# Edge stage of a graph network: tile pairs that share a PSUM bank, and float32r parts in place of bfloat16 parts and float32

## The chip, the cores and the metric

The kernel runs on one core of a Trainium2 chip. The metric is the device time of one launch in microseconds (us); lower is better. Engines are named as in the profile: PE is TensorE (its matmuls), PEld its weight loads, DVE is VectorE, ACT is ScalarE, POOL is GpSimd and SP is SyncE.

## The reference

Two graph network layers run on N = 3125 nodes with 256 features and E = 50000 edges with 16 features each. The change touches the first:

```
h   = relu(layernorm(x))
m   = relu(concat(h[src], h[dst], edge_attr) @ mW1 + mb1)     # 50000 x 512
agg = segment_sum(m @ mW2 + mb2, src)                          # per source node
u   = relu(concat(h, agg) @ uW1 + ub1) @ uW2 + ub2
x   = x + h + u
```

The second layer is three graph convolutions (matmul, sum over neighbours, gelu) and a residual; the change does not touch its code.

## The kernel before

The kernel runs four stages one after the other, each a block in which every engine has an instruction stream of its own and the streams meet at semaphores.

1. `sort_and_embed` sorts the edges by block of 128 source nodes (25 blocks) and scatters them, 128 at a time, into a list in DRAM (`src_list`); a tile is 128 edges of one source block. It also computes A = h @ mW1[source rows] + mb1 and B = h @ mW1[target rows] for all nodes. B goes to DRAM, A stays in SBUF, cut into three bfloat16 parts per value (`a_part`).
2. `edge_mlp`, the stage that the change rewrites, walks over NT = 416 tiles. For tile t:
   - SP loads the edge rows, POOL gathers the 128 rows of B for the targets (`brow`, a ring of 8 buffers, freed by the add of eight tiles earlier).
   - DVE makes the one-hot of the edges' place in their source block, once in bfloat16 (`oh16`, L1017) and once in float32 (`oh32`, L1018).
   - PE transposes the one-hot and the edge features ("turn", L953 and L954), ACT copies both to SBUF (L984 and L986, `turned`).
   - PE computes the "edge" sum in a PSUM bank: features times weights (L962), then the transposed one-hot times the three parts of A (L964).
   - DVE adds the gathered rows of B (L1025, `pre`), ACT applies relu (L992, `hid`).
   - PE computes the "node" sum: one-hot (float32) times `hid` (float32), L971, which the trace shows as two matmul records; DVE adds it into the sum of the source block, `S` (L1011).

   PE's order per step is turn(t), edge(t-1), node(t-2). ACT's order is the copies of t, relu of t-1. DVE's order is the S add of t-4, the one-hots of t, the B add of t-2. `pTurn`, `pEdge`, `pNode`, `turned`, `pre` and `hid` have two buffers each. Before the first tile DVE sets all of `S` (12800 columns) to zero, L997.
3. `build_and_update` counts edges for the second layer in a dense matrix and runs the node update; it reads `S`.
4. `graph_layers` is the second layer.

Of the kernel before, what the change touches and what calls it, by code (L numbers as in the profile page):

```python
# [40 lines left out]
NT = -(-E // P) + NW  # L41
NS = -(-(NT + NW * (CHK - 1)) // 8) * 8
LT = NT + 2 + NW
FULL_TILES = -(-E // P)
# [14 lines left out]
assert COLS * P >= E and COLS * P - E <= 2 * P and BLOCKS * CH == COLS and NT % 16 == 0 and CHK * CW >= NW * P  # L59
# [8 lines left out]
def windows(nc, eng, tile_map, first, n):  # L68

    _, got = nc.values_load_multi_w_load_instructions(  # L70
        tile_map[0:1, first:first + n], engines=[eng.engine], min_val=0, max_val=NW - 1,
        skip_runtime_bounds_check_because="the map counts at most NW - 1 windows before a tile")
    return {first + k: w for k, w in enumerate(got)}
# [30 lines left out]
def sort_and_embed(nc, io, dr, keep):  # L104
# [3 lines left out]
    with ExitStack() as stack:  # L108
        g = Names(nc, stack)
        hi16 = [g.sb(f"hi16_{n}", [P, COLS], BF16) for n in range(2)]  # L110
        ck_i32 = g.sb("ck_i32", [P, COLS], I32)
        lo16 = [g.sb(f"lo16_{n}", [P, COLS], BF16) for n in range(2)]
        onehot_dst = g.sb("onehot_dst", [P, 2, NW, CH], BF16)
        FILL = (NT - FULL_TILES) * ROW
        early = keep.A[:, NW * 3 * HID - (WINS + CHK + 6) * COLS - 2 * (CH + 3) * BINS - 2 * FILL:NW * 3 * HID]
# [13 lines left out]
        ck = g.sb("ck", [P, COLS])  # L129
# [16 lines left out]
        start_x = g.sb("start_x", [1, 2, WINS, CHK])  # L146
# [4 lines left out]
        base_row = g.sb("base_row", [P, BINS])  # L151
        ck_i = g.sb("ck_i", [P, WINS, CHK], I32)
        ck_row = g.sb("ck_row", [P, BINS])
        step_i = g.sb("step_i", [P, NS], I32)
        step_f = g.sb("step_f", [P, NS])
# [6 lines left out]
        ended_w = ended[0:NW - 1, 0, 0:NT]  # L162
# [17 lines left out]
        last_f = g.sb("last_f", [1, NW])  # L180
        some_w = g.sb("some_w", [1, NW])
        spare = g.sb("spare", [1, NW])
        iota_i = g.sb("iota_i", [P, P], I32)
        bins_i = g.sb("bins_i", [P, BINS], I32)
# [5 lines left out]
        stats = g.sb("stats", [P, NW, 6])  # L190
# [4 lines left out]
        h = g.sb("h", [P, 2, D])  # L195
        hT = g.sb("hT", [P, 2, D])
        w1 = g.sb("w1", [P, 4, HID])
        b1 = g.sb("b1", [1, HID])
        rA = g.sb("rA", [P, HID])
# [3 lines left out]
        we_r = rA[0:EF, :]  # L203
# [55 lines left out]
        ra_ready = g.sem("ra_ready")  # L259
        a_mid = g.sem("a_mid")  # L260
# [10 lines left out]
        def a_part(w, k):  # L271
            return keep.A[:, w * (3 * HID) + k * HID:w * (3 * HID) + (k + 1) * HID]
# [4 lines left out]
        def _(sp):  # L277
# [10 lines left out]
            def load_feat(m):  # L288
# [17 lines left out]
            sp.dma_start(dr.src_list[:, FULL_TILES:NT, :], fill[:, :, :]).then_inc(filled, 16)  # L306
# [6 lines left out]
            sp.wait_ge(filled, 16)  # L313
            _, last = nc.values_load_multi_w_load_instructions(
                last_w[0:1, :], engines=[sp.engine], min_val=0, max_val=LT - 1,
                skip_runtime_bounds_check_because="a source block's last tile, or a spare one of its own")
            for w in range(0, NW, 2):
                sp.dma_start(dr.src_list[:, bass.ds(last[w], 1), :], fill[:, 0:1, :]).then_inc(last_filled, 16)
# [51 lines left out]
        def _(act):  # L370
# [23 lines left out]
            def middle_parts(k):  # L394
# [7 lines left out]
            act.wait_ge(filled, 16)  # L402
            _, last = nc.values_load_multi_w_load_instructions(
                last_w[0:1, :], engines=[act.engine], min_val=0, max_val=LT - 1,
                skip_runtime_bounds_check_because="a source block's last tile, or a spare one of its own")
            for w in range(1, NW, 2):
                act.dma_start(dr.src_list[:, bass.ds(last[w], 1), :], fill[:, 0:1, :]).then_inc(last_filled, 16)
            for k in range(BLOCKS):
# [14 lines left out]
                if odd == 0 and 0 <= s - 1 < NW:  # L423
                    w = s - 1
                    act.wait_ge(a_done, w + 1)
                    nc.scalar.copy(a_part(w, 0), pA[:, :]).then_inc(a_hi, 1)
                    act.wait_ge(ra_ready, w + 1)
                    nc.scalar.copy(a_part(w, 1), rA[:, :]).then_inc(a_mid, 1)
# [21 lines left out]
        def _(dve):  # L450
# [34 lines left out]
            v.tensor_scalar(spare[:, :], keep.iota[0:1, 0:NW], float(NT + 2), None, ALU.add).then_inc(consts, 1)  # L485
# [19 lines left out]
            dve.wait_ge(consts, 3 + CH)  # L505
# [20 lines left out]
            link(v.tensor_scalar(tiles_i[:, :], sum_all, float(P - 1), None, ALU.add))  # L526
            link(v.tensor_scalar(tiles_i[:, :], tiles_i[:, :], 7, None, ALU.arith_shift_right))
            link(v.tensor_copy(tiles_f[:, :], tiles_i[:, :]))
# [6 lines left out]
            link(v.scalar_tensor_tensor(out=last_f[:, :], in0=tiles_end[0:1, 0:NW], scalar=-1.0, in1=spare[:, :],  # L535
                                        op0=ALU.add, op1=ALU.subtract))
            link(v.tensor_scalar(some_w[:, :], tiles_f[0:1, 0:NW], 0.0, None, ALU.is_gt))
            link(v.tensor_tensor(last_f[:, :], last_f[:, :], some_w[:, :], ALU.mult))
            v.tensor_tensor(last_w[:, :], last_f[:, :], spare[:, :], ALU.add).then_inc(last_ready, 1)
            v.tensor_copy(bin_iota[:, :], bins_i[:, :]).then_inc(consts, 1)  # L540
            v.tensor_scalar(before16[:, :], keep.iota[:, :], part[:, 0:1], None, ALU.is_gt).then_inc(consts, 1)
            dve.wait_ge(consts, 5 + CH)
# [8 lines left out]
            dve.wait_ge(consts, 12 + CH)  # L551
# [94 lines left out]
            def tables(k):  # L646

                if k == 5:
                    link(v.tensor_tensor(diag_w[:, :], tiles_end[0:NW, 0:NW], keep.ident[0:NW, 0:NW], ALU.mult))
                    link(v.tensor_reduce(end_w[:, :], diag_w[:, :], AX.X, ALU.add))  # L650
                    v.tensor_scalar(ended_w, step_f[0:NW - 1, 0:NT], end_w[0:NW - 1, 0:1], None, ALU.is_ge
                                    ).then_inc(tables_ready, 1)
                if k == 7:
                    dve.wait_ge(tables_done, 1)
                    link(v.tensor_copy(keep.src_map[:, :], pH[0:1, 0:NT]))
# [65 lines left out]
            for k in range(BLOCKS):  # L721
# [16 lines left out]
                if odd == 0 and 0 <= s - 1 < NW:  # L738
                    w = s - 1
                    dve.wait_ge(a_hi, w + 1)  # L740
                    if w == 0:
                        dve.wait_ge(we_parts, 1)
                    v.tensor_tensor(rA[:, :], pA[:, :], a_part(w, 0), ALU.subtract).then_inc(ra_ready, 1)
# [17 lines left out]
        def _(pe):  # L761
# [47 lines left out]
            def tables(k):  # L809
                if k == 6:  # L810
                    pe.wait_ge(tables_ready, 1)
                    mm(pH[:, 0:NT], ones[0:NW - 1, :], ended_w, start=True, stop=True).then_inc(tables_done, 1)
# [17 lines left out]
            for k in range(BLOCKS):  # L830
                if k == 0:
                    pe.wait_ge(base_copied, 1)
                    pe.wait_ge(consts, 5 + CH)
                    before(0)
                    pe.wait_ge(consts, 6 + CH)
                if k == 2:
                    pe.wait_ge(consts, 12 + CH)
# [25 lines left out]
                if odd == 1 and 0 <= s < NW:  # L863
                    if s == 0:
                        pe.wait_ge(w_in, 48)
                    if s >= 1:
                        pe.wait_ge(ra_ready, s)
# [10 lines left out]
def edge_mlp(nc, io, dr, keep):  # L878


    with ExitStack() as stack:
        g = Names(nc, stack)
        S = keep.S
        T = 16
        LCS = T // LC
        rows = g.sb("rows", [P, LCS, LC, ROW])
        BR = 8
# [5 lines left out]
        oh16 = g.sb("oh16", [P, 4, P], BF16)  # L893
        oh32 = g.sb("oh32", [P, 4, P])
        turned = g.sb("turned", [P, 2, 2 * P], BF16)
        pre = g.sb("pre", [P, 2, HID])
        hid = g.sb("hid", [P, 2, HID])
# [4 lines left out]
        s_zero = g.sem("s_zero")  # L902
# [8 lines left out]
        hid_ready = g.sem("hid_ready")  # L911
        node_done = g.sem("node_done")
        s_added = g.sem("s_added")
        GRP = 8
# [27 lines left out]
        def _(pe):  # L942
            mm = nc.tensor.matmul
            win = windows(nc, pe, keep.src_map, 0, GRP)

            for t in range(NT + 2):
                j = t % T
                if inside(t, NT):

                    pe.wait_ge(oh_ready, 2 * t + 2)  # L950
                    if t >= 2:
                        pe.wait_ge(turn_copied, t - 1)
                    nc.tensor.transpose(pT[j % 2][:, 0:P], oh16[:, j % 4, :], keep.ident16[:, :])  # L953
                    nc.tensor.transpose(pT[j % 2][0:EW, P:2 * P], rows16[:, j // LC, j % LC, 4:4 + EW],  # L954
                                        keep.ident16[:, :]).then_inc(turn_done, 1)
                if inside(t - 1, NT):
                    b = (t - 1) % 2
                    pe.wait_ge(turn_copied, t)
                    if t >= 3:
                        pe.wait_ge(pre_ready, t - 2)  # L960
                    w = win[t - 1]
                    mm(pE[b][:, :], turned[0:EW, b, P:2 * P], keep.we[:, :], start=True, stop=False)  # L962
                    for k in range(3):
                        last = mm(pE[b][:, :], turned[:, b, 0:P], keep.A[:, bass.ds(w * (3 * HID) + k * HID, HID)],  # L964
                                  start=False, stop=(k == 2))
                    last.then_inc(edge_done, 1)
                if inside(t - 2, NT):
                    pe.wait_ge(hid_ready, t - 1)
                    if t >= 4:
                        pe.wait_ge(s_added, t - 3)  # L970
                    mm(pN[t % 2][:, :], oh32[:, (t - 2) % 4, :], hid[:, t % 2, :], start=True, stop=True  # L971
                       ).then_inc(node_done, 1)
# [851 lines left out]
```

## Time and profile before

| | us |
|---|---|
| median of 3 runs | 2334.24 (2333.3 to 2336.12) |
| the profiled execution, its own time | 2332.68 |
| its span | 2330.9 |
| edge stage, first to last add into S | 600.94 to 1369.8 |

Of the span PE is busy 2022.8 us, DVE 1688.7, POOL 1178.0 and ACT 807.3. The busy time of an engine over the whole span is an average over four stages with different limits, so the stage has to be read by itself: a window inside it, and the order and the starts of its instructions on each engine. Matmuls overlap one another, so what one costs is the distance from its start to the next one's start, not its duration.

### The profile page before, as it was taken

How to read it: one execution, taken by the hardware profiler on the slowest of the kernel's cores; microseconds unless marked ns; L12 is line 12 of the kernel's file. 1: busy time of each engine (PE TensorE's matmuls, PEld its weight loads, DVE VectorE, ACT ScalarE, POOL GpSimd, SP SyncE). 2: the span in 40 equal slices, each digit the busy share in tenths (PEclk: the TensorE clock that was granted, in tenths of full speed). 3: DMA queues.
4: the chain of work that ended last, by engine and by line, in shares of the span. 5: the costliest groups of instructions: out<-in, count | busy, mean ns of one | idle time of the engine just before them, and what ended most of it. 6: DMA issues, size and time to landing. Idle time of an engine off the chain costs nothing. (4 is left out here: it accounts for less than half of the span.)

```text
span 2330.9 us, 37075 instructions
## 1 busy us (share of the span) xinstructions
PE 2022.8 (87%) x9567; PEld 1299.8 (56%) x9567; DVE 1688.7 (72%) x5368; ACT 807.3 (35%) x2430; POOL 1178.0 (51%) x1453
## 2 busy tenths in 40 slices
PE   4666766662799999999999989999977999999998
PEld 2333433331344444444444447777756898898897
DVE  7987776663899999999999977777764454454454
ACT  0222121110455555555555545555543201101100
POOL 3777777776555555555555549989862100000000
PEclk7677666665899999999999999999997999999999
DMA  4111111111555555555555541111122343343353
GB/s 115 46 46 46 46 45 46 46 45 33 146 155 158 156 157 156 156 157 156 158 156 158 156 150 60 60 56 60 62 67 74 99 138 108 91 138 108 99 144 109
DMA packets 185586, 242.59 MB, mean 104 GB/s; under 512 B 26333, under 2 KB 154266, under 8 KB 185387
## 3 DMA queue, kind: packets, MB, share of 16 engines
q0 software_dynamic: 45968, 119.96, 18.3%
q1 hardware_dynamic: 108258, 94.94, 14.1%
q10 hardware_dynamic: 31160, 25.32, 3.3%
q8 instruction: 90, 1.47, 0.3%
q14 instruction: 110, 0.89, 0.1%
HBM read 195.17 MB, written 44.86 MB: 103 GB/s over the span
## 5 line engine op out<-in xcount | busy, mean ns | idle before, releaser
L936 POOL DMA_INDIRECT brow<-B_rows,rows x416 | 396.4, 953 | 354.3 <-DVE pre L1025 343.5
L362 POOL DMA_INDIRECT src_list<-ring,ring_row x392 | 411.8, 1051 | 153.6 <-issue 116.8
L1706 PE MATMUL pO<-F,y 128*128 128x448 f32 x2100 | 455.7, 372 | 13.9 <-DVE y L1595 11.6
L971 PE MATMUL pNode<-hid,oh 128*128 128x512 f32 x832 | 430.4, 599 | 0.7 <-ACT hid L992 0.6
L1706 PEld LDWEIGHTS pO<-F,y 128*128 128x128 f32 x2100 | 394.6, 188 | 49.0 <-DVE y L1595 13.4
L992 ACT ACTIVATE hid<-pre 128x512 f32<-128x512 f32 x416 | 262.1, 630 | 342.3 <-DVE pre L1025 342.3
L1011 DVE TENSOR_TENSOR S<-S,pNode 128x512 f32 x416 | 286.1, 688 | 72.9 <-PE pNode L971 54.7
L964 PE MATMUL pEdge<-A,turned 128*128 x1248 | 338.8, 379 | 0.0
L1566 DVE CAST F<-raw 128x448 fp32r<-128x448 uint16 x525 | 204.4, 392 | 173.5 <-PE pO L1706 169.3
L1141 POOL TENSOR_SCALAR src_oh<-iota,src_s 128x128 bf16<-128x128 bf16 x473 | 304.5, 659 | 27.4 <-PE pC L1310 26.0
L1025 DVE TENSOR_TENSOR pre<-pEdge,brow 128x512 f32<-128x512 f32 x416 | 281.4, 676 | 3.4 <-PE pEdge L964 3.3
L795 PE MATMUL pP<-U,upto 128*128 128x182 bf16 x385 | 60.0, 322 | 161.3 <-DVE posf L557 161.1
L971 PEld LDWEIGHTS pNode<-hid,oh 128*128 128x128 f32 x832 | 136.8, 188 | 88.5 <-ACT hid L992 79.5
L1185 DVE TENSOR_SCALAR dst_oh<-iota_cw,dst_s 128x458 bf16<-128x458 f16 x568 | 183.0, 375 | 0.0
L964 PEld LDWEIGHTS pEdge<-A,turned 128*128 128x128 bf16 x1248 | 122.0, 98 | 101.2 <-issue 1.4
L1310 PE MATMUL pC<-dst_oh,src_oh 128*128 128x458 bf16 x568 | 157.8, 361 | 13.8 <-DVE dst_oh L1185 5.9
L962 PE MATMUL pEdge<-we_rows,turned 96*128 96x512 bf16 x416 | 159.0, 382 | 0.2 <-ACT turned L986 0.2
L795 PEld LDWEIGHTS pP<-U,upto 128*128 128x128 bf16 x385 | 42.9, 127 | 203.7 <-DVE posf L557 191.1
L1017 DVE TENSOR_SCALAR oh<-iota,rows 128x128 bf16<-128x128 bf16 x416 | 153.1, 368 | 0.9 <-DVE S L997 0.9
L1397 ACT CAST c_rows<-pC 128x458 uint16<-128x458 f32 x175 | 94.6, 540 | 155.1 <-PE pC L1310 150.5
L1018 DVE TENSOR_SCALAR oh<-iota,rows 128x128 f32<-128x128 f32 x416 | 146.1, 351 | 0.0
L953 PEld LDWEIGHTS pTurn<-ident,oh 128*128 128x128 bf16 x416 | 39.9, 96 | 177.4 <-DVE oh L1018 176.9
(280 smaller groups left out, 2914.6 us busy)
## 6 DMA issues: line engine op xcount, KB each, us to landing
raw<-C_rows SPq DMA_DIRECT2D x105, 560.0 KB, 3.8
C_rows<-c_rows ACTq DMA_DIRECT2D x175, 114.5 KB, 1.7
rows<-src_list SPq DMA_DIRECT2D x104, 100.0 KB, 2.4
brow<-B_rows,rows POOLq DMA_INDIRECT x416, 3.4
B_rows<-bst SPq DMA_DIRECT2D x25, 256.0 KB, 2.1
src_list<-ring,ring_row POOLq DMA_INDIRECT x392, 2.2
hT_rows<-hT SPq DMA_DIRECT2D x25, 128.0 KB, 1.8
resid<-in_x_dram SPq DMA_DIRECT2D x1, 3072.0 KB
```

What stands on the lines that cost most here:

```text
L362: nc.gpsimd.indirect_dma_start(dr.src_list[:, :, :].rearrange("p t w -> (p t) w"), bass.IndirectOffsetOnAxis(ap=ring_row[:, k % RING, t:t ...
L936: nc.gpsimd.indirect_dma_start(brow[:, t % BR, :], None, dr.B, bass.IndirectOffsetOnAxis(ap=rows_i[:, b, j, 1:2], axis=0)).then_inc(b_in[t ...
L962: mm(pE[b][:, :], turned[0:EW, b, P:2 * P], keep.we[:, :], start=True, stop=False)
L964: last = mm(pE[b][:, :], turned[:, b, 0:P], keep.A[:, bass.ds(w * (3 * HID) + k * HID, HID)], start=False, stop=(k == 2))
L971: mm(pN[t % 2][:, :], oh32[:, (t - 2) % 4, :], hid[:, t % 2, :], start=True, stop=True).then_inc(node_done, 1)
L992: nc.scalar.activation(hid[:, b, :], pre[:, b, :], ACT.Relu).then_inc(hid_ready, 1)
L1011: v.tensor_tensor(sw, sw, pN[j % 2][:, :], ALU.add).then_inc(s_added, 1)
L1025: v.tensor_tensor(pre[:, b, :], pE[b][:, :], brow[:, (j - 2) % BR, :], ALU.add).then_inc(pre_ready, 1)
L1141: nc.gpsimd.tensor_scalar(src_oh[:, s % SLOTS, :], keep.iota16[:, :], src_s[:, s:s + 1], None, ALU.is_equal).then_inc(src_ready, 1)
L1185: v.tensor_scalar(dst_oh[:, s % SLOTS, :], iota_cw[:, :], dst_s[:, s:s + 1], None, ALU.is_equal).then_inc(dst_ready, 1)
L1566: v.tensor_copy(F[:, n % FS, 0:CHUNK], raw[:, m % RAWS, n % RAWW, 0:CHUNK]).then_inc(f_ready, 1)
L1706: last = mm(pO[n % 2][half][:, 0:CHUNK], y_part(win, part, half), F[:, (n * NW + win) % FS, 0:CHUNK], start=(win == 0 and part == 0), stop ...
```

## The change

It does four things in the edge stage, and changes what lies around it to fit.

- A is kept in two float32r parts per value instead of three bfloat16 parts. PE's edge sum is then three matmuls, not four. `turned` is float32r, and the transposed edge features have a buffer of their own.
- Tiles go in pairs of the same source block. The node sums of both tiles accumulate in one PSUM bank, and DVE adds once per pair, with one instruction that multiplies the running sum by 0 or 1 (`going_on`) and adds the bank. So no large memset is needed. Each source block has an even number of tiles, and NT becomes 440.
- In every fourth tile (t % 4 == 1) relu is split into two float32r parts: ACT writes the upper part, DVE computes max(pre, 0) - upper, and the node sum is two float32r matmuls instead of one float32 matmul.
- DVE makes one one-hot per tile (float32r, 8 buffers). The transpose on PE reads the upper half of each 32-bit value, a bfloat16 with a step of two. PE's node sum runs one step later: turn(t), edge(t-1), node(t-3).

The first stage loses the middle part of A (one ACT copy and one DVE subtraction per source block) and writes its filler tiles with two DMAs instead of one. The third stage finds its weights in other places of SBUF and loads `uW1` with two DMAs instead of one.

```
-NT = -(-E // P) + NW
+PAIRS = E // (2 * P) + NW
+NT = 2 * PAIRS
...
-                    v.tensor_tensor(rA[:, :], pA[:, :], a_part(w, 0), ALU.subtract).then_inc(ra_ready, 1)
+                    v.tensor_tensor(a_part(w, 1), pA[:, :], a_part(w, 0).bitcast(F32), ALU.subtract).then_inc(a_lo, 1)
...
-                if odd == 1 and 0 <= s - 1 < NW:
-                    w = s - 1
-                    dve.wait_ge(a_mid, w + 1)
-                    v.tensor_tensor(a_part(w, 2), rA[:, :], a_part(w, 1), ALU.subtract).then_inc(a_lo, 1)
...
+            def turn(t):
+                pe.wait_ge(oh_ready, t + 1)
+                if t >= 2:
+                    pe.wait_ge(turn_copied, t - 1)
+                nc.tensor.transpose(pT[t % 2][:, 0:P], oh_upper[:, t % OHS, :, 1], keep.ident16[:, :])
+                nc.tensor.transpose(pT[t % 2][0:EW, P:2 * P], rows16[:, (t // LC) % LCS, t % LC, 4:4 + EW],
+                                    keep.ident16[:, :]).then_inc(turn_done, 1)
+
+            def edge(t):
+                pe.wait_ge(turn_copied, t + 1)
+                if t >= 2:
+                    pe.wait_ge(pre_ready, t - 1)
+                mm(pE[t % 2][:, :], turned_e[:, t % 2, :], keep.we[:, :], start=True, stop=False)
+                for k in range(2):
+                    last = mm(pE[t % 2][:, :], turned[:, t % 2, :],
+                              keep.A[:, 2 * HID + k * HID:][:, bass.ds(at[t // 2], HID)], start=False, stop=(k == 1))
+                last.then_inc(edge_done, 1)
+
+            def node(t):
+                pe.wait_ge(hid_ready, t + 1)
+                first, p = t % 2 == 0, t // 2
+                if first and p >= 2:
+                    pe.wait_ge(pair_added, p - 1)
+                if in_parts(t):
+                    mm(pN[p % 2][:, :], oh[:, t % OHS, :], upper[:, :], start=first, stop=False)
+                    pe.wait_ge(lower_ready, parts_upto(t))
+                    last = mm(pN[p % 2][:, :], oh[:, t % OHS, :], lower[:, :], start=False, stop=not first)
+                else:
+                    last = mm(pN[p % 2][:, :], oh[:, t % OHS, :].bitcast(F32), whole[(t % 4 + 1) // 2][:, :], start=first,
+                              stop=not first)
+                last.then_inc(node_done, 1)
...
+            for t in range(NT + 1):
+                if t < NT:
+                    act.wait_ge(turn_done, t + 1)
...
+                    nc.scalar.activation(turned[:, t % 2, :], pT[t % 2][:, 0:P], ACT.Copy,
                                          accum_out=keep.tile_deg[:, t:t + 1])
+                    nc.scalar.copy(turned_e[:, t % 2, :], pT[t % 2][0:EW, P:2 * P]).then_inc(turn_copied, 1)
+                u = t - 1
+                if u >= 0:
+                    act.wait_ge(pre_ready, u + 1)
...
+                    to = upper[:, :] if in_parts(u) else whole[(u % 4 + 1) // 2][:, :]
+                    nc.scalar.activation(to, pre[:, u % 2, :], ACT.Relu).then_inc(hid_ready, 1)
...
-            v.memset(S[:, :], 0.0).then_inc(s_zero, 1)
+            v.memset(keep.sums[:, 0:HID], 0.0).then_inc(start_ready, 1)
...
+            def lower_part(t):
+                dve.wait_ge(hid_ready, t + 1)
...
+                v.scalar_tensor_tensor(out=lower[:, :], in0=pre[:, t % 2, :], scalar=0.0, in1=upper[:, :].bitcast(F32),
+                                       op0=ALU.max, op1=ALU.subtract).then_inc(lower_ready, 1)
+
+            def add_pair(p):
+                dve.wait_ge(node_done, 2 * p + 2)
...
+                v.scalar_tensor_tensor(out=keep.sums[:, bass.ds(at[p], HID)],
+                                       in0=keep.sums[:, bass.ds(at[max(p - 1, 0)], HID)],
+                                       scalar=keep.going_on[:, p:p + 1], in1=pN[p % 2][:, :],
+                                       op0=ALU.mult, op1=ALU.add).then_inc(pair_added, 1)
+
+            one_hot(0)
+            for t in range(NT + 6):
+                if t + 1 < NT:
+                    one_hot(t + 1)
+                if 0 <= t - 2 < NT:
+                    add_target(t - 2)
+                if 0 <= t - 3 < NT and in_parts(t - 3):
+                    lower_part(t - 3)
+                if t >= 6 and t % 2 == 0:
+                    p = (t - 6) // 2
...
+                    add_pair(p)
...
-            sp.dma_start(uw1[:, :, :], io["L0_gnn_uW1"].rearrange("(k p) n -> p k n", p=P)).then_inc(w_in, 16)
+            for half in range(2):
+                sp.dma_start(uw1[:, 4 * half:4 * half + 4, :],
+                             io["L0_gnn_uW1"][:, half * D:(half + 1) * D].rearrange("(k p) n -> p k n", p=P)
+                             ).then_inc(w_in, 16)
```

## Rows read from the trace of the kernel before

**Rows 1.** Windows: each engine's busy time and instructions in a stretch, then PE's clock.

```profile
core 0: us, PE busy (x) PEld busy (x) DVE busy (x) ACT busy (x) POOL busy (x), PEclk, DMA share, GB/s
100.00:300.00 200.00, 142.44 (x618) 76.27 (x616) 158.62 (x759) 42.46 (x98) 155.18 (x148) 0.70 0.16 47
...
900.00:1100.00 200.00, 200.00 (x866) 89.35 (x866) 181.81 (x434) 111.66 (x435) 108.26 (x136) 1.00 0.56 157
...
1400.00:1736.00 336.00, 309.58 (x1870) 235.72 (x1868) 255.78 (x874) 180.34 (x333) 304.60 (x472) 1.00 0.19 60
```

**Rows 2.** Timeline of PE over one tile: start, duration, line, operation.

```profile
1000.79 0.22 PE L953 MATMUL pTurn<-ident,oh 128*128 128x128 bf16 x1
...
1000.90 0.38 PE L962 MATMUL pEdge<-we_rows,turned 96*128 96x512 bf16 x1
1001.12 0.81 PE L964 MATMUL pEdge<-A,turned 128*128 x3
1001.77 1.02 PE L971 MATMUL pNode<-hid,oh 128*128 128x512 f32 x2
1002.63 0.22 PE L953 MATMUL pTurn<-ident,oh 128*128 128x128 bf16 x1
```

**Rows 3.** Timeline of DVE over the same stretch and a little on.

```profile
1001.10 0.69 DVE L1011 TENSOR_TENSOR S<-S,pNode 128x512 f32 x1 [0.24 <-PE pNode L971]
1001.70 0.39 DVE L1017 TENSOR_SCALAR oh<-iota,rows 128x128 bf16<-128x128 bf16 x1
1001.86 0.29 DVE L1018 TENSOR_SCALAR oh<-iota,rows 128x128 f32<-128x128 f32 x1
1002.08 0.67 DVE L1025 TENSOR_TENSOR pre<-pEdge,brow 128x512 f32<-128x512 f32 x1
...
1005.85 0.67 DVE L1025 TENSOR_TENSOR pre<-pEdge,brow 128x512 f32<-128x512 f32 x1
1006.62 0.69 DVE L1011 TENSOR_TENSOR S<-S,pNode 128x512 f32 x1
```

**Rows 4.** Timeline of ACT over the same stretch.

```profile
1002.78 0.63 ACT L992 ACTIVATE hid<-pre 128x512 f32<-128x512 f32 x1 [0.85 <-DVE pre L1025]
1003.32 0.26 ACT L984 ACTIVATE turned<-pTurn 128x128 bf16<-128x128 bf16 x1
...
1003.57 0.25 ACT L986 COPY turned<-pTurn 96x128 bf16<-96x128 bf16 x1
```

**Rows 5.** Timeline of all engines at the start of the edge stage.

```profile
582.87 10.72 DVE L997 MEMSET S<- 128x12800 f32 x1 [34.92 <-issue]
583.78 0.96 POOL L936 DMA_INDIRECT brow<-B_rows,rows  x1 [0.30 <-issue]
...
595.72 0.25 ACT L986 COPY turned<-pTurn 96x128 bf16<-96x128 bf16 x1
...
596.03 0.61 PE L962 MATMUL pEdge<-we_rows,turned 96*128 96x512 bf16 x1 [0.25 <-ACT turned L986]
...
596.43 1.49 PE L964 MATMUL pEdge<-A,turned 128*128 x3
...
597.95 0.69 DVE L1025 TENSOR_TENSOR pre<-pEdge,brow 128x512 f32<-128x512 f32 x1 [2.26 <-PE pEdge L964]
```

**Rows 6.** Chain of waits, second layer: 25 float32r matmuls in a row.

```profile
1828.17 5.69 PE pT_g L1741 x25
```

**Rows 7.** Single lines: durations of one in ns, min/median/max, then the shapes.

```profile
L1741 PEld LDWEIGHTS pT_g<-y,pick x75: 187/188/188, 1827.8 to 2188.3; 128*128 128x128 f32 x75
```

**Rows 8.** Single lines with scalar_tensor_tensor on DVE, same columns.

```profile
L674 DVE SCALAR_TENSOR_TENSOR A<-A x1: 351/351/351, 136.6 to 136.6; 128x182 f32<-128x182 f32 x1
L1595 DVE SCALAR_TENSOR_TENSOR y<-pY,dis,y x75: 479/484/485, 1780.1 to 2181.6; 128x256 fp32r<-128x256 f32 x75
```

**Rows 9.** DMA issues by queue: count, size, median us from issue to landing.

```profile
brow<-B_rows,rows POOLq DMA_INDIRECT x416, 3.4
```

**Rows 10.** Timeline of SP at the start of the third stage.

```profile
1371.28 0.43 SPq L1243 DMA_DIRECT2D A<-in_L_gnn_uW_dram  x1
```

More of the change, by code:

```diff
@@ L65, in inside, with blocks_of @@
     return 0 <= t < n
-def windows(nc, eng, tile_map, first, n):
+def blocks_of(nc, eng, table, first, n):
     _, got = nc.values_load_multi_w_load_instructions(
-        tile_map[0:1, first:first + n], engines=[eng.engine], min_val=0, max_val=NW - 1,
-        skip_runtime_bounds_check_because="the map counts at most NW - 1 windows before a tile")
+        table[0:1, first:first + n], engines=[eng.engine], min_val=0, max_val=(NW - 1) * 2 * HID,
+        skip_runtime_bounds_check_because="the map counts at most NW - 1 source blocks before a pair of tiles")
     return {first + k: w for k, w in enumerate(got)}
@@ L312, in _ @@
             sp.wait_ge(last_ready, 1)
-            sp.wait_ge(filled, 16)
+            sp.wait_ge(filled, 32)
             _, last = nc.values_load_multi_w_load_instructions(
-                last_w[0:1, :], engines=[sp.engine], min_val=0, max_val=LT - 1,
-                skip_runtime_bounds_check_because="a source block's last tile, or a spare one of its own")
+                last_w[0:1, :], engines=[sp.engine], min_val=0, max_val=NT - 2,
+                skip_runtime_bounds_check_because="the first tile of a source block's last pair")
             for w in range(0, NW, 2):
-                sp.dma_start(dr.src_list[:, bass.ds(last[w], 1), :], fill[:, 0:1, :]).then_inc(last_filled, 16)
+                sp.dma_start(dr.src_list[:, bass.ds(last[w], 2), :], fill[:, 0:2, :]).then_inc(last_filled, 16)
             def store_b(w):
@@ L401, in _ @@
             act.wait_ge(last_ready, 1)
-            act.wait_ge(filled, 16)
+            act.wait_ge(filled, 32)
             _, last = nc.values_load_multi_w_load_instructions(
-                last_w[0:1, :], engines=[act.engine], min_val=0, max_val=LT - 1,
-                skip_runtime_bounds_check_because="a source block's last tile, or a spare one of its own")
+                last_w[0:1, :], engines=[act.engine], min_val=0, max_val=NT - 2,
+                skip_runtime_bounds_check_because="the first tile of a source block's last pair")
             for w in range(1, NW, 2):
-                act.dma_start(dr.src_list[:, bass.ds(last[w], 1), :], fill[:, 0:1, :]).then_inc(last_filled, 16)
+                act.dma_start(dr.src_list[:, bass.ds(last[w], 2), :], fill[:, 0:2, :]).then_inc(last_filled, 16)
             for k in range(BLOCKS):
@@ L911, in edge_mlp, with in_parts, parts_upto, before_same @@
         hid_ready = g.sem("hid_ready")
+        lower_ready = g.sem("lower_ready")
         node_done = g.sem("node_done")
-        s_added = g.sem("s_added")
-        GRP = 8
+        pair_added = g.sem("pair_added")
+        def in_parts(t):
+            return t % 4 == 1
+        def parts_upto(t):
+            return sum(in_parts(u) for u in range(t + 1))
+        def before_same(t):
+            return t - 2 if in_parts(t) and in_parts(t + 2) else t - 4
         block = stack.enter_context(nc.Block())
@@ L943, in _ @@
             mm = nc.tensor.matmul
[L944 to L972, printed above, removed]
-                if t % GRP == 0 and 0 < t < NT:
-                    win.update(windows(nc, pe, keep.src_map, t, GRP))
@@ L976, in _ @@
+            pe.wait_ge(start_ready, 1)
+            for t in range(NT + 3):
+                if t < NT:
+                    turn(t)
+                if 0 <= t - 1 < NT:
+                    edge(t - 1)
+                if 0 <= t - 3 < NT:
+                    node(t - 3)
+                if t % (2 * GRP) == 0 and 0 < t < NT:
+                    at.update(blocks_of(nc, pe, keep.pair_at, t // 2, min(GRP, PAIRS - t // 2)))
         @block.scalar
@@ L1030, in build_and_update @@
+            dve.wait_ge(pair_added, PAIRS)
 def build_and_update(nc, io, dr, keep):
```

242 lines of the change are left out of this document (119 added, 123 removed).

## The prediction

> **What bounds the kernel now.** I read the windows view first, because the share of busy time over the whole span mixes four stages. In the middle of the edge stage PE is busy all of 200 us at full clock, DVE 182, ACT 112, POOL 108 [rows 1]. PE makes eight matmuls per tile, so 866 in 200 us are 108.2 tiles, 1.848 us a tile, and 416 tiles take 768.8 us.
>
> Then the timeline of PE over one tile, for the distances between starts [rows 2]: two transposes 0.11, features 0.22, three parts of A 0.65 (0.217 each), node sum 0.86, next tile. That is 1.84 without a gap, so PE's own work is the bound. The edge sum is complete 0.16 after the node sum has begun (1001.12 + 0.81 = 1001.93 against 1001.77).
>
> DVE is close behind [rows 3]: from one start to the next 0.60 (S add), 0.16, 0.22 (one-hots), then the B add; after a B add the S add starts 0.77 later although the former lasts 0.67, so an operand at a register's address costs 0.10 more. ACT follows a B add after 0.70 (1002.08 to 1002.78) and needs 0.54 + 0.25 + 0.25 until both copies are done [rows 4].
>
> The first stage is bound by POOL: 155.2 us busy and 148 issues of 0.30 (the wait that stands before POOL's gather [rows 5]) fill 200 [rows 1].
>
> **The change, part by part.** S(t) is the start of PE's step t: turn(t), edge(t-1), node(t-3).
>
> *PE's own work.* 25 float32r matmuls of 512 columns take 5.69 us, 0.228 each [rows 6]; their weight load of 0.188 hides under them [rows 7]. Edge: 0.22 + 2 x 0.228 = 0.675 instead of 0.87. Node: 0.86 in three tiles of four, 2 x 0.228 = 0.455 in the fourth. A step is 0.11 + 0.675 + 0.86 = 1.645, the step with the parts (t % 4 == 0) is 1.24. Four steps make 6.175, or 1.544 a tile. The strided weight load of the transpose isn't in the trace; a slower one (0.19 as in [rows 7]) still lies under the node matmul before it, so I take nothing, at most 0.09 a tile.
>
> [...]
>
> *DVE's work.* Per four tiles: four one-hots (0.22), four B adds (0.60), one lower part, two pair adds. The last two are scalar_tensor_tensor. One over 182 columns of float32 from SBUF takes 0.351, which is 182 cycles at 0.96 per ns (0.19) plus 0.16; over 512 columns that makes 0.53 + 0.16 = 0.69. The one with a PSUM operand and a pointer takes 0.484 for 256, so 0.75 for 512 [rows 8]. The next instruction starts 0.09 before the end, as behind the S add (0.69, 0.60) [rows 3]. In all 0.88 + 2.4 + 0.60 + 2 x (0.66 + 0.10) = 5.4 of PE's 6.175. As a sum it fits.
>
> *The order on DVE doesn't fit.* In step 4 (any step with t % 4 == 0) its queue holds one_hot(5), add(2), lower(1), pair add, then in step 5 one_hot(6), add(3). Yet this is the step in which PE is fastest. Behind add(3) hangs relu(3) on ACT, and ACT takes the copies of tile 5 only after relu(3); edge(5) needs them. I follow this chain from S(3):
> - edge(2) done and seen by DVE: 0.11 + 0.675 + 0.16 = 0.945, plus 0.03 (matmul end 597.92, DVE 597.95 [rows 5]) = 0.975
> - add(2) to lower(1) 0.60; lower(1) to the pair add 0.69 + 0.10 = 0.79; to one_hot(6) 0.66; to add(3) 0.22
> - add(3) to relu(3) 0.70; relu and both copies 1.04; to PE 0.06 (595.97 to 596.03 [rows 5])
>
> The sum is 5.045. PE by itself would reach edge(5) after 1.645 + 1.24 + 1.645 + 0.11 = 4.64. So PE waits 0.405 in step 6, once in four tiles, and the next round starts from there: no other link is longer. relu(4) starts about S(3) + 5.0, its copies of tile 6 are ready near 6.1, and edge(6) comes at 6.7. The lower part is ready near S(3) + 2.3, PE asks at 2.65. Four tiles take 6.175 + 0.405 = 6.58, 1.645 a tile; **440 tiles take 723.8 us, 45.0 less** than 768.8, although they are 24 more.
>
> Bounds: with both scalar_tensor_tensor at the price of a plain add (0.60 to the next) the chain is 0.25 shorter: 1.583 a tile, 696.4. Upwards I know of DVE's register loads (five per eight tiles, not visible before, where eight were) and of the pair add's second register address; another 0.22 on the chain gives 1.70 a tile, 748.
>
> *The memset.* It lasts 10.72 for 12800 columns; for 512 it is 0.43. All of the stage's start hangs on it: from its end to the first B add are 4.4 us [rows 5]. The gathers don't take its place, since POOL's run beside the memset (tile 1 issued at 583.78 [rows 5]) and land after 3.4 [rows 9], before the new first add at about 587.7. **10.3 less.** If something else took over, the nearest candidate is that landing, 587.2, so nothing is lost.
>
> *Ends.* The node sum runs a step later and the last add is a pair's: 0.8 more (0 to 2). In the third stage one more DMA at SP lies before the weights that DVE and PE wait for, 0.43 [rows 10]: 0.5 more (0 to 1.5, its rows being shorter). The copies of A and the DVE work that leave the first stage are worth nothing, as POOL's scatter covers them; without that cover they would be 25 x 0.6 = 15 us of DVE. The second filler DMA at its start delays POOL by 1 at most, against four short DVE instructions fewer: nothing. POOL in the edge stage gets less time per tile (1.645 for a gather of 0.96 + 0.30) and still has room; the same for SP's loads, with eight tiles of B rows ahead.
>
> **Sum.** -45.0 - 10.3 + 0.8 + 0.5 = -54.0, against the profiled execution's own 2332.7: 2278.7, say **2279 us**. That execution is 1.6 below the median, which changes nothing. By the bounds the forecast case spans 2251 to 2303.
>
> **Rivals.**
> - *PE stays the bound.* DVE's sum is below PE's, and my chain is only 0.4 longer than PE's path; if ACT's or DVE's links are shorter when nothing waits, the stage runs at 1.544 to 1.58: 679.3 to 696, the kernel 2234 to 2251. For it: all links but one have room. Against it: every link is a row. Chance 0.18.
> - *DVE is later than the chain says.* Register loads in the queue, or a pair add that waits for the node sum and pushes the next one-hot. At 1.70 to 1.75 a tile: 2303 to 2325. Chance 0.18.
> - *The lower part costs twice as much and ends the gain.* If the instruction takes half an element a cycle, it lasts 1.22, the chain gets 0.53 longer, four tiles take 7.11, a tile 1.778, 440 tiles 782: 2337, on the line between no change and slower. It decides from 0.49 us more per four tiles on (1.768 a tile). The same for the pair adds too would be 0.53 more: 1.91, 840, so 2395. Against both: neither row of scalar_tensor_tensor shows half rate, 0.351 for 182 columns with both tensors in SBUF would have to be 0.54 [rows 8]. Chances 0.07 (0.04 of it no change, 0.03 slower) and 0.02. The Trainium skill states it as a rule (Vector Engine (DVE) Microarchitecture Reference, Points that are easy to get wrong): this instruction "with two non-bf16 SBUF sources halves throughput". The trace disagrees by that row, at 182 columns; it has none at 512.
> - *The clock falls.* With PE waiting, the granted clock could drop to 1.2 GHz as in the first stage (0.70 with PE busy 142 of 200); PE's 6.175 would double, 440 tiles take 1359: 2914. But in the third stage PE is busy 310 of 336 at 1.00 [rows 1], 92%, and here it would be 6.175 of 6.58, 94%. Chance 0.03.
>
> **How the numbers follow.** The forecast case has 0.52. Faster by over 0.2% (about what a measurement of this kernel tells from none): 0.52 + 0.18 + 0.18 = 0.88. Within 0.2%: 0.04. Slower: 0.03 + 0.02 + 0.03 = 0.08. The range of 8 in 10 takes the forecast case, the upper two thirds of the first rival and most of the second: 2240 to 2318.
>
> **What the changed profile would show.** PE about 94% busy in the stage, with one wait of some 0.4 us in four tiles, at the feature matmul of every tile with t % 4 == 1, released by ACT's copy. ACT's relu of t % 4 == 3 starts late after DVE. The lower part lasts 0.69, the pair add 0.75. The first B add comes near 588. PE fully busy would mean the first rival; waits at more places the second; a lower part of 1.2 the third. The prediction is wrong at its root if float32r matmuls start more than 0.23 apart, if the strided transpose shows, or if the first stage becomes longer.

## The result

| | before | after |
|---|---|---|
| median | 2335.2 (2333.3 to 2338.3, 4 runs) | 2258.15 (2256.8 to 2260.0, 4 runs) |
| span of the profiled execution | 2330.9 | 2254.8 |
| first to last B add | 768.5 (415 tiles) | 705.9 (439 tiles) |

The ratio is 0.967, interval 0.965 to 0.969: faster, 77 us. The forecast was 2279, the range 2240 to 2318.

The windows view of the changed kernel, same three stages as [rows 1], and one longer stretch of the edge stage:

```profile
core 0: us, PE busy (x) PEld busy (x) DVE busy (x) ACT busy (x) POOL busy (x), PEclk, DMA share, GB/s
100.00:300.00 200.00, 143.09 (x619) 76.78 (x617) 153.76 (x754) 35.86 (x87) 155.49 (x147) 0.69 0.16 47
900.00:1100.00 200.00, 199.59 (x876) 119.94 (x874) 167.25 (x344) 126.20 (x501) 130.73 (x157) 1.00 0.64 180
1320.00:1656.00 336.00, 309.61 (x1870) 235.84 (x1867) 254.93 (x874) 180.34 (x333) 305.25 (x472) 1.00 0.18 60
...
700.00:1200.00 500.00, 498.91 (x2184) 299.19 (x2182) 417.39 (x858) 314.74 (x1248) 327.02 (x390) 1.00 0.65 181
```

PE's and POOL's rows have changed only in the edge stage; DVE and ACT have a little less in the first. PE shows as busy nearly all the time, but this hides its wait: a matmul is counted until its modelled end, which covers a short gap before the next. The wait is in the starts. Timeline of PE over four tiles (the turn begins a step; L970 and L972 are the edge sum, L986 the whole node sum, L982 and L984 its two parts):

```profile
1001.09 0.22 PE L962 MATMUL pTurn<-ident,oh 128*128 128x128 bf16 x1
...
1002.74 0.22 PE L962 MATMUL pTurn<-ident,oh 128*128 128x128 bf16 x1
...
1003.54 0.39 PE L982 MATMUL pNode<-hid_upper,oh 128*128 128x512 f32 x1
1003.77 0.39 PE L984 MATMUL pNode<-hid_lower,oh 128*128 128x512 f32 x1
1004.00 0.23 PE L962 MATMUL pTurn<-ident,oh 128*128 128x128 bf16 x1
...
1005.66 0.22 PE L962 MATMUL pTurn<-ident,oh 128*128 128x128 bf16 x1
...
1005.95 0.39 PE L970 MATMUL pEdge<-we_rows,turned_e 96*128 96x512 bf16 x1
...
1007.50 0.22 PE L962 MATMUL pTurn<-ident,oh 128*128 128x128 bf16 x1
```

The steps are 1.65, 1.26, 1.66 and 1.84. In the last one the features' matmul begins 0.29 after the turn and not 0.11: 0.18 of wait at edge(5), where the prediction has it. The view of waits counts it (columns: engine, line and releaser; us in total, times, longest), over 700 to 1200, which holds 312 tiles:

```profile
DVE pre L1039 <- PE pEdge L972: 53.5, 116, 0.8
DVE sums L1054 <- PE pNode L986: 29.1, 39, 0.8
...
PEld pEdge L970 <- ACT turned_e L1010: 12.1, 76, 0.2
```

76 times is once in four tiles. DVE over the same stretch (L1030 one-hot, L1039 B add, L1045 lower part, L1054 pair add):

```profile
998.59 0.69 DVE L1039 TENSOR_TENSOR pre<-pEdge,brow 128x512 f32<-128x512 f32 x1
1000.03 0.75 DVE L1054 SCALAR_TENSOR_TENSOR sums<-sums,going_on,pNode 128x512 f32 x1 [0.75 <-PE pNode L986]
...
1002.09 0.69 DVE L1039 TENSOR_TENSOR pre<-pEdge,brow 128x512 f32<-128x512 f32 x1 [0.31 <-PE pEdge L972]
1002.69 0.68 DVE L1045 SCALAR_TENSOR_TENSOR hid_lower<-pre,hid_upper 128x512 fp32r<-128x512 f32 x1
1003.29 0.74 DVE L1054 SCALAR_TENSOR_TENSOR sums<-sums,going_on,pNode 128x512 f32 x1
1003.95 0.29 DVE L1030 TENSOR_SCALAR oh<-iota,rows 128x128 fp32r<-128x128 f32 x1
1004.15 0.68 DVE L1039 TENSOR_TENSOR pre<-pEdge,brow 128x512 f32<-128x512 f32 x1
```

This is the predicted queue, from the B add at 1002.09 to the B add at 1004.15. The distances from start to start are 0.60, 0.60, 0.66, 0.20; the prediction had 0.60, 0.79, 0.66, 0.22. ACT's copies for edge(5) end at 1005.90 (L1010, from 1005.65). The chain from 1001.09 to 1005.95 is 4.86, predicted 5.045. Ahead of the pair add at 1000.03 DVE is idle for 0.75, once in eight tiles (39 times above); the profile puts it down to the node matmul, though the last one before it had ended at 999.41 (L986, from 998.39). The experiments come back to that row.

The start of the edge stage, from the same kernel's timeline:

```profile
574.63 0.48 DVE L1022 MEMSET sums<- 128x512 f32 x1 [32.38 <-PEq L109]
...
576.89 1.01 POOL L948 DMA_INDIRECT brow<-B_rows,rows  x1 [0.15 <-issue]
...
580.34 0.69 DVE L1039 TENSOR_TENSOR pre<-pEdge,brow 128x512 f32<-128x512 f32 x1 [2.94 <-DMA brow<-B_rows,rows]
```

Where 76.1 us of span went, by four pieces that fill it:

| piece | before | after | difference | predicted |
|---|---|---|---|---|
| to the first stage's last scatter | 569.4 | 563.7 | -5.7 | 0 |
| from there to the first B add | 28.6 | 16.7 | -11.9 | -10.3 |
| to the last B add | 768.5 | 705.9 | -62.6 | -45.0 |
| to the end | 964.5 | 968.6 | +4.1 | +1.3 |

### The profile page after: what moved, and what is told of

Its sections match the earlier page's. It is cut to its first block and busy times, and to the rows that moved or that the text cites. A ratio compares the mean times of both kernels' runs of the same rounds, so it can differ in the third digit from the quotient of the medians.

```text
span 2254.8 us, 35599 instructions
## 1 busy us (share of the span) xinstructions
PE 1954.4 (87%) x9319; PEld 1379.4 (61%) x9319; DVE 1555.3 (69%) x4889; ACT 806.8 (36%) x2501; POOL 1219.9 (54%) x1483
## 5 line engine op out<-in xcount | busy, mean ns | idle before, releaser
L948 POOL DMA_INDIRECT brow<-B_rows,rows x440 | 439.4, 999 | 237.3 <-DVE pre L1039 211.9
L1753 PEld LDWEIGHTS pO<-F,y 128*128 128x128 f32 x2100 | 395.6, 189 | 48.1 <-DVE y L1642 13.5
L972 PE MATMUL pEdge<-A,turned 128*128 x880 | 360.3, 491 | 0.0
L1039 DVE TENSOR_TENSOR pre<-pEdge,brow 128x512 f32<-128x512 f32 x440 | 302.9, 688 | 81.9 <-PE pEdge L972 78.2
L986 PE MATMUL pNode<-hid_whole,oh 128*128 128x512 f32 x660 | 338.3, 594 | 0.2
L1017 ACT ACTIVATE hid_whole<-pre 128x512 f32<-128x512 f32 x330 | 208.6, 632 | 160.0 <-DVE pre L1039 159.9
L1054 DVE SCALAR_TENSOR_TENSOR sums<-sums,going_on,pNode 128x512 f32 x220 | 163.4, 743 | 42.2 <-PE pNode L986 42.0
L972 PEld LDWEIGHTS pEdge<-A,turned 128*128 128x128 f32 x880 | 170.3, 194 | 11.0 <-issue 0.2
L970 PE MATMUL pEdge<-we_rows,turned_e 96*128 96x512 bf16 x440 | 170.0, 386 | 2.9 <-ACT turned_e L1010 1.4
L395 ACT CAST ring<-feat 128x336 bf16<-128x336 f32 x56 | 26.3, 470 | 368.2 <-DMA src_list<-ring,ring_row 342.7
L986 PEld LDWEIGHTS pNode<-hid_whole,oh 128*128 128x128 f32 x660 | 125.0, 190 | 29.1 <-ACT hid_whole L1017 0.9
L962 PE MATMUL pTurn<-ident,oh 128*128 128x128 bf16 x440 | 98.1, 223 | 35.5 <-DVE oh L1030 35.5
```

The costliest lines, as they stand in the source:

```text
L948: nc.gpsimd.indirect_dma_start(brow[:, t % BR, :], None, dr.B, bass.IndirectOffsetOnAxis(ap=rows_i[:, b, j, 1:2], axis=0)).then_inc(b_in[t ...
L970: mm(pE[t % 2][:, :], turned_e[:, t % 2, :], keep.we[:, :], start=True, stop=False)
L972: last = mm(pE[t % 2][:, :], turned[:, t % 2, :], keep.A[:, 2 * HID + k * HID:][:, bass.ds(at[t // 2], HID)], start=False, stop=(k == 1))
L986: last = mm(pN[p % 2][:, :], oh[:, t % OHS, :].bitcast(F32), whole[(t % 4 + 1) // 2][:, :], start=first, stop=not first)
L1017: nc.scalar.activation(to, pre[:, u % 2, :], ACT.Relu).then_inc(hid_ready, 1)
L1039: v.tensor_tensor(pre[:, t % 2, :], pE[t % 2][:, :], brow[:, t % BR, :], ALU.add).then_inc(pre_ready, 1)
```

## The experiments

Ratios are to the kernel before on the same chip; "the stage" is the time from the first to the last B add in the profile, 705.9 in the changed kernel, 439 tiles.

**1. The parts at another place.** The tile whose relu is split is the one with t % 4 == 2, so that the lower part falls into a step without a pair add.

```
 def in_parts(t):
-    return t % 4 == 1
+    return t % 4 == 2
...
-    ... whole[(t % 4 + 1) // 2]
+    ... whole[(0, 1, 1, 2)[t % 4]]
```

> The split tile moves from t % 4 == 1 to t % 4 == 2, so that the lower part stands on DVE in a step without a pair add. Theory A (the chain edge(2), B add, lower part, pair add, one-hot, B add, relu, copies, edge(5), 4.86 us in the changed kernel's trace, holds PE up by 0.18 in four tiles): the longest chain is then 4.24 against PE's 4.69, no wait is left, four tiles take 6.24 instead of 6.42, 110 x 0.18 = 20 us less: 2238. Rival B (PE's own work or its weight loads make that gap): nothing changes, 2258. Rival C (DVE as a whole is the limit): nothing changes either, but the wait moves to another tile.

Measured 2260.3, ratio 0.969 (0.967 to 0.970); the stage 706.1. No gain where 2238 was expected: with the lower part and the pair add in different steps, something else holds PE too. The waits over 700 to 1200 and the place where it happens:

```profile
DVE sums L1054 <- issue: 29.1, 39, 0.8
...
PE pEdge L970 <- ACT turned_e L1010: 9.9, 39, 0.3
```

```profile
999.86 0.69 DVE L1039 TENSOR_TENSOR pre<-pEdge,brow 128x512 f32<-128x512 f32 x1 [0.17 <-PE pEdge L972]
1001.29 0.75 DVE L1054 SCALAR_TENSOR_TENSOR sums<-sums,going_on,pNode 128x512 f32 x1 [0.75 <-issue]
```

PE now waits 39 times and not 76, once in eight tiles, but longer: the turns lie at 1001.78, 1003.44, 1005.52, 1006.77, so one step is 2.08 where 1.66 is its own work. That is 0.42 in eight tiles, 55 times, 23 us. Ahead of it stands the same idle of 0.75 before a pair add, and here the profile names no releaser. In the code DVE loads five registers at this point, every fourth pair (`blocks_of` in DVE's loop); this is what the expectations call the burst. The trace has it as one instruction of DVE's sequencer (`DVEq`), which isn't counted as busy. The view of its line over 700 to 1200 in the changed kernel (duration in ns, min/median/max):

```profile
L71 DVEq TENSOR_LOAD <-pair_at x39: 1180/1183/1193, 703.6 to 1191.0; - x39
```

The one before the pair add at 1000.03 begins at 998.6 and lasts 1.18, so it ends 0.24 before that pair add and 0.4 after the node matmul. The row of the changed kernel was put down to the wrong cause. Here the load begins at 999.9 and ends 0.24 before the pair add as well. Four tiles take 6.23 from turn to turn where no such load stands and 6.65 where one does, so the theory is right in the rounds without a load.

**2. No parts.** `in_parts` returns False, `whole` has four buffers, and DVE's B add no longer waits for a lower part.

```
-    return t % 4 == 1
+    return False
...
-    ... whole[(t % 4 + 1) // 2]
+    ... whole[t % 4]
...
-                    dve.wait_ge(lower_ready, parts_upto(t - 2))
```

> No tile is split; all node sums are float32 matmuls, four buffers for relu's result. Theory A: PE's own work is 4 x 1.66 = 6.64 per four tiles and nothing waits: 0.22 more, 110 x 0.22 = 24 us more: 2282. If the split buys nothing, because PE then only waits: 2258.

Measured 2280.9, ratio 0.977 (0.975 to 0.978); the stage 729.4, 6.65 per four tiles, which is four times PE's 1.66.

```profile
700.00:1200.00 500.00, 499.56 (x2109) 292.76 (x2109) 366.06 (x754) 311.15 (x1207) 301.71 (x377) 1.00 0.61 174
```

PE is the bound, with 2 waits in 500 us. The parts are worth 22.8 us. The rest of the stage's gain fits A in two parts (PE's step is 1.66, and was 1.84); no run tests A alone.

**3. Parts in every second tile,** odd ones and even ones.

```
-    return t % 4 == 1
+    return t % 2 == 1        # the other run: t % 2 == 0
...
-    ... whole[(t % 4 + 1) // 2]
+    ... whole[t % 4 // 2]
```

> Every second tile is split (t % 2 == 1), so lower part and pair add stand together in every even step. PE's own work is 5.84 per four tiles. Theory A: the same chain now closes a loop of 5.98 (B add to edge(5) 3.86, edge(5) to edge(6) 1.25, to the B add 0.87), so 0.44 less than 6.42 and 48 us less: 2210. Rival C (DVE's sum, 5.72 per four tiles by the distances, is in truth larger): 6.2 or more, 2234 or above.

> Every second tile is split, but the even ones (t % 2 == 0), so lower parts and pair adds stand in different steps. PE's own work is 5.84, DVE's 5.72, both as in the run with odd tiles. Theory A: the longest chain is 4.13 against PE's 4.18, so PE is never held up: 5.84 per four tiles, 64 us less than the changed kernel: 2194. Rival C (only DVE's sum counts, not its order): the same time as the run with odd tiles.

Measured 2248.1 (ratio 0.963, 0.961 to 0.965) and 2237.5 (0.959, 0.957 to 0.960); the stage 694.4 and 686.6. Both are faster than the change, and both miss what the chain forecast, 2210 and 2194. The rival by which only DVE's sum counts had the same time for both, and they differ by 10.6. The turns show where the chain is right. With odd parts four tiles take 6.06 in the rounds without a burst (turns at 1003.26 and 1009.32; 5.98 expected) and 6.58 in those with one (996.68 to 1003.26); with even parts 5.87 (1002.71 to 1008.58; 5.84 expected) and 6.65 (996.06 to 1002.71). The waits of the even one:

```profile
DVE sums L1054 <- issue: 30.3, 40, 0.8
...
PE pNode L984 <- DVE hid_lower L1045: 20.8, 40, 0.5
```

Again DVE is idle for 0.76, 40 times, and again PE is late once in eight tiles, now at the node sum's second part.

**4. The registers loaded one at a time.** This tests the theory that the first experiment left: the load of five costs DVE 0.75. With the parts at t % 4 == 2, DVE loads one register per pair, in the odd steps, behind the one-hot.

```
+    if t % 2 == 1 and 0 <= t - 5 < NT:
+        at.update(blocks_of(nc, dve, keep.pair_at, (t - 5) // 2, 1))
     if 0 <= t - 2 < NT:
         add_target(t - 2)
...
-        if p % GRP == 0:
-            first = max(p - 1, 0)
-            at.update(blocks_of(nc, dve, keep.pair_at, first, min(p + GRP, PAIRS) - first))
```

> The parts at t % 4 == 2, as in the run of 2260, and DVE's register loads one at a time, each in an odd step ahead of the B add that waits for PE, where that run had five in a burst ahead of the pair add. Theory R (the burst keeps DVE for 0.75 us once in eight tiles, and with the parts at t % 4 == 2 PE waits for it): PE's own work is the bound again, 6.24 per four tiles, 20 us less: 2238 to 2242. Theory D (DVE has too much work in a row by itself, the loads cost what the trace shows as idle anyway): 2256 to 2262. If one load costs nearly what five cost together, two in four tiles would make it 2265 to 2275.

Measured 2238.1, ratio 0.958 (0.956 to 0.960); the stage 685.4, 6.245 per four tiles.

```profile
700.00:1200.00 500.00, 500.00 (x2250) 304.61 (x2249) 431.23 (x883) 332.46 (x1287) 336.97 (x402) 1.00 0.66 186
```

The idle before the pair add and PE's wait are gone from the list of waits, and four tiles take PE's own 6.24. The 22 us that experiment 1 had missed are here. Only the loads differ, in eight tiles four of one register in place of one of five: it was the burst. The same view of the loads, in this run and then in the kernel before, whose load was of eight registers:

```profile
L71 DVEq TENSOR_LOAD <-pair_at x161: 299/304/323, 700.6 to 1198.8; - x161
```

```profile
L70 DVEq TENSOR_LOAD <-src_map x33: 593/596/606, 711.4 to 1185.3; - x33
```

A load of one takes 0.30, of five 1.18 and of eight 0.60; PE's own, of four, takes 0.33 in the changed kernel. So it isn't a price per register, and why five are dearer than eight was not tested, nor a load of four or eight on DVE at this place.

**5. The burst on the chain.** The changed kernel with the burst two steps earlier, between the lower part and the pair add of the queue shown above.

```
-        if p % GRP == 0:
+        if p == 0 or p % GRP == GRP - 1:
```

> The changed kernel with the burst of register loads moved by two steps: it stands between the lower part and the pair add, in the chain on which edge(5) waits, instead of two steps from there. As many loads as before but one more in the first burst. Theory R (the 0.75 us of idle ahead of the pair add once in eight tiles are the loads, and the changed kernel hides them): now they lie on the chain, 55 times 0.75 = 41 us more than 2258: 2290 to 2299. Rival W (that idle is a wait for the node matmul, as the profile puts it down, and the loads cost next to nothing): 2256 to 2262.

Measured 2274.3, ratio 0.974 (0.972 to 0.976); the stage 725.9, 20 us longer. The rival without a cost falls; the size, 41 expected on top of 2258, was wrong by half. DVE where the burst stands, and the load there:

```profile
1010.82 0.69 DVE L1039 TENSOR_TENSOR pre<-pEdge,brow 128x512 f32<-128x512 f32 x1 [0.77 <-PE pEdge L972]
1011.43 0.68 DVE L1045 SCALAR_TENSOR_TENSOR hid_lower<-pre,hid_upper 128x512 fp32r<-128x512 f32 x1
1012.36 0.75 DVE L1054 SCALAR_TENSOR_TENSOR sums<-sums,going_on,pNode 128x512 f32 x1 [0.24 <-issue]
```

```profile
L71 DVEq TENSOR_LOAD <-pair_at x1: 1181/1181/1181, 1010.9 to 1010.9; - x1
```

The pair add starts 0.93 after the lower part, and 0.60 without a burst: 0.33 lost, not 0.75. The load begins 0.1 after the B add's start and ends at 1012.12, and the pair add starts 0.24 later, as in the changed kernel and in experiment 1. What differs is how much work DVE's array has meanwhile: here the B add and the lower part, there the B add alone, so it is idle for 0.24 here and for 0.75 there. 55 times 0.33 are 18 of the 20 us. The round without a burst takes 6.42 in this run (turns at 1003.41 and 1009.83). In the changed kernel every round does, with a burst or without (turns at 996.33, 1002.74 and 1009.16, the burst in the first; 12.86 per eight tiles over the stage), so there the burst costs nothing: it stands ahead of B adds that wait for PE anyway. The changed kernel without its burst was not measured.

**6. Both: parts in every even tile, loads one at a time.** The diffs of 3 and 4 together.

> The parts in every even tile, as in the run of 2237.5, with DVE's register loads one at a time in the odd steps. Per four tiles DVE has 4 x 0.22 + 4 x 0.60 + 2 x 0.60 + 2 x 0.66 = 5.80, PE has 5.8 too; that run took about 6.2. Theory R: without the burst (0.37 per four tiles) it comes down to 5.9 to 6.1 per four tiles: 2200 to 2225. Theory D (DVE is full and a single load costs about as much as the burst): no gain or a loss, 2236 to 2260.

Measured **2197.4**, ratio 0.941 (0.939 to 0.943); the stage 646.9, below the range expected.

```profile
1000.05 0.68 DVE L1039 TENSOR_TENSOR pre<-pEdge,brow 128x512 f32<-128x512 f32 x1
1000.65 0.68 DVE L1045 SCALAR_TENSOR_TENSOR hid_lower<-pre,hid_upper 128x512 fp32r<-128x512 f32 x1
1001.25 0.28 DVE L1030 TENSOR_SCALAR oh<-iota,rows 128x128 fp32r<-128x128 f32 x1
1001.52 0.69 DVE L1039 TENSOR_TENSOR pre<-pEdge,brow 128x512 f32<-128x512 f32 x1
1002.12 0.73 DVE L1054 SCALAR_TENSOR_TENSOR sums<-sums,going_on,pNode 128x512 f32 x1
...
1005.89 0.68 DVE L1039 TENSOR_TENSOR pre<-pEdge,brow 128x512 f32<-128x512 f32 x1
```

```profile
700.00:1200.00 500.00, 500.00 (x2393) 316.67 (x2391) 500.00 (x1025) 353.01 (x1366) 407.41 (x428) 1.00 0.70 197
```

Four tiles take 5.84 on DVE with no gap, and PE's own work is 2 x (1.66 + 1.26) = 5.84 as well; the mean of the stage is 5.89. Single loads, 0.30 each, cost nothing visible: they run while DVE's array is busy. This is the fastest version, 61 us below the change, and PE and DVE are both full. Against the version of experiment 3 the eight tiles are 12.51 - 11.79 = 0.72 shorter, the burst's idle.

**7. The start hangs on DVE.** Twenty more memsets of 512 columns in a chain ahead of the one that is left.

```
+    for n in range(20):
+        link(v.memset(keep.sums[:, 0:HID], 0.0))
     v.memset(keep.sums[:, 0:HID], 0.0).then_inc(start_ready, 1)
```

> Twenty more memsets of 512 columns stand ahead of the one on which the edge stage's start hangs, each behind the other. Together with the last one they are to last about 10 us (21 x 0.48), nearly as long as the one memset of the kernel before (10.72). Theory M (the edge stage's start came earlier because the memset is short): the time of 10 us comes back, 2268 against the changed kernel's 2258. Rival N (PE's or the gathers' start sets the first B add, and the long memset was hidden under the first gather for the most part): 2258 to 2262.

Measured 2267.5, ratio 0.971 (0.969 to 0.973): 9.4 more than the change. They take more than the 10 expected, as each starts 0.66 after the last: 578.86 to 592.50 in the timeline, 13.6. The first B add is released by PE again:

```profile
592.02 0.48 DVE L1025 MEMSET sums<- 128x512 f32 x1 [0.17 <-DVE sums L1024]
...
595.21 0.69 DVE L1042 TENSOR_TENSOR pre<-pEdge,brow 128x512 f32<-128x512 f32 x1 [2.04 <-PE pEdge L972]
```

From the last scatter to the first B add are 27.3, and 16.7 in the changed kernel. So 13.2 more of memset move the first B add by 10.6. The stage itself is 2.2 shorter (703.7; argued: the gathers are ahead by then), and the whole comes to 8.5, near the 9.4 of the medians.

**Without a time.** Four more runs were planned and gave no time: A's second part multiplied twice, which would price A on PE; the changed kernel with its registers loaded one at a time; and the kernel before for a second and a third profile. On the second question see the rounds in experiment 5; the others stay open.

## Why the prediction was right, and where it was off

**PE's own work: right.** Steps of 1.65 and 1.26 where 1.645 and 1.24 were forecast, 6.24 where 6.175; 0.065 in four tiles, 7 us too little over 440. The float32r parts start 0.23 apart (1003.54, 1003.77), and the strided transpose's weight load doesn't show. That PE alone makes 6.65 without parts is experiment 2.

**The order on DVE: the mechanism right, one term mis-sized.** PE waits at edge(5), once in four tiles, after the queue that the prediction lists. The term that failed is "lower(1) to the pair add 0.69 + 0.10 = 0.79"; measured 0.60. Two errors lie in it. The 0.10 came from the 0.77 between the B add and the S add in [rows 3], read as the price of a register's address. It was a wait. PE in the kernel before:

```profile
1005.44 1.03 PE L971 MATMUL pNode<-hid,oh 128*128 128x512 f32 x2
```

This node sum ends at 1006.47, and the S add starts 0.15 later, at 1006.62; in the four tiles before, the S add starts 0.14 or 0.15 after a node sum's end too. In the pair add, with two register addresses and no wait, nothing of the 0.10 is left. The 0.69 was the duration worked out from [rows 8] without the 0.09 by which the next instruction starts before the end, which the same paragraph had stated. With 0.60, and the others' small differences, the chain is 4.86 and the wait 0.18, not 0.405: 0.225 x 110 = 24.8 us less. Less 7.2 for PE's steps, this is 17.6, the whole difference between -45.0 and -62.6. The kernel so came out between the forecast case and its lower bound (2251), where this very term had been priced as a plain add.

**The lower part at half rate: refuted at 512 columns.** The row that the trace before did not have:

```profile
L1045 DVE SCALAR_TENSOR_TENSOR hid_lower<-pre,hid_upper x110: 680/682/685, 584.3 to 1284.9; 128x512 fp32r<-128x512 f32 x110
```

Both tensors are 32 bits wide and in SBUF, and it takes 682, against 688 of the B add. Against the rule cited from the Trainium skill (Vector Engine (DVE) Microarchitecture Reference, Points that are easy to get wrong), the measurement decides; 1.22 was its price.

**DVE later by its register loads: true as a mechanism, not in this kernel.** The prediction named the loads as an upward bound and in the second rival, and took five to be no more visible than the eight before. The load of five lasts 1.18 where that of eight lasted 0.60. It leaves DVE idle for 0.75 in eight tiles, and experiments 1 and 4 show what that can cost (22 us). That it costs nothing here is luck: the change happens to put it where DVE waits for PE.

**The memset: -10.3 forecast, -11.9 to the first B add.** Two terms that the prediction had at nothing lie in it. DVE reaches its memset sooner after the last scatter, 10.9 instead of 13.5 (cause open), and from the memset's end to the first B add are 5.2 instead of 4.4. The releaser is the gather (580.34, issued 576.89: 3.45), which the prediction had as "the nearest candidate" at no cost. In experiment 7, where PE is the last again, it is 2.7. Experiment 7 gives back 9.4 with a memset chain somewhat longer than the old memset. That some of the start's gain is lost again within the stage is read from one pair of profiles, not tested by itself.

**The first stage: 0 forecast, -5.7 in the two profiles, cause open.** The nine profiles of kernels with the changed first stage, one code, have the last scatter at 563.6 to 567.9, and the first at 36.7 to 39.3. The profile before has 569.4 and 39.3. So up to 4.3 are within what one execution differs from another, and with one profile of before the rest can't be settled.

**The end: +1.3 forecast, +4.1.** Of the 4.1, 2.9 lie in the stretch between the third and the fourth stage. The chain of waits has there a piece that it calls issue, first before, then after:

```profile
1736.17 28.35 issue
```

```profile
1656.45 31.27 issue
```

And the windows over it, of before and of after:

```profile
1736.00:1750.00 14.00, 6.96 (x24) 5.57 (x24) 4.48 (x18) 1.17 (x2) 0.00 (x0) 0.52 0.22 66
1750.00:1764.00 14.00, 11.89 (x56) 10.46 (x55) 10.71 (x42) 3.59 (x7) 0.00 (x0) 0.74 0.01 1
```

```profile
1656.00:1670.00 14.00, 6.24 (x21) 4.99 (x22) 4.28 (x18) 1.17 (x2) 0.00 (x0) 0.50 0.26 67
1670.00:1684.00 14.00, 12.48 (x46) 10.56 (x45) 7.96 (x32) 3.59 (x7) 0.00 (x0) 0.50 0.00 0
```

The granted clock rose to 2.4 GHz within the second stretch before and stayed at 1.2 GHz after. Of the 2.9 us, 2.5 lie in the matmuls that run there (L1662 to L1666 before, from 1743.00 to 1756.42; the same ones after, from 1663.71 to 1679.60) and 0.4 ahead of the first of them. The other 1.2 of the 4.1 are near the forecast 1.3. The changed kernels have 966.9 to 969.5 from the last B add to the end; the shortest is one in which the clock rose early too. Whether the change makes this likelier can't be told from one profile of before.

**The clock in the edge stage** stayed at 1.00, also in experiment 3's odd version, where PE is busy 477 of 500.

## What to carry to other kernels

When two engines are both near full, follow the chain through the slower engine's queue from start to start, and price every link by start-to-start distances of rows in which nothing was waited for; a distance that holds a wait looks like a cost (0.77 here), and one that forgets the overlap adds 0.09 each time. Register loads belong into that queue, and their durations are in the trace under the line that loads, though no busy time counts them: one load of five took 1.18 and left the engine idle for 0.75, loads of one took 0.30 and were hidden, and the profile put the idle down to a matmul in one kernel. If an experiment that should gain does not, look for idle that comes at the period of a loop's block (39 times in 312 tiles) before you give up the theory: here that turned 2260 into 2238 and led to 2197.

## What was not expected of the hardware

- DVE's load of five registers lasts 1.18, of one 0.30, of eight 0.60. After the load of five the pair add starts 0.24 later. DVE's array works on meanwhile with what it already has, so the idle is 0.75 or 0.24 (experiments 1 and 5), and none with single loads (experiments 4 and 6).
- A gather's issue on POOL lasts longer when it begins inside a lower part: 1.35 at 1000.81 and 0.95 at 1002.47 in the fastest version, whose mean is 1135 ns; the mean before is 953, without parts 952. Between 620 and 1200, the 198 gathers that begin inside a lower part take 1.31 to 1.37 and the other 198 take 0.94 to 0.96. With parts in the odd tiles, where gathers begin before it, the mean is 961. POOL had room for that here; the cause wasn't tested.
- Small memsets in a chain start 0.66 apart at a duration of 0.48.
